# A vision transformer tower: probability transposes by row halves, exponential ahead of one eviction, value mask on VectorE

## The chip, the cores and the metric

The kernel runs on one core of a Trainium2 chip. The metric is device time in microseconds (us) of one execution; the time before is the median of three. The profile is that of one further execution. Engines are named as in the profile: PE is TensorE's matmul array, PEld its weight load, DVE is VectorE, ACT is ScalarE, POOL is GpSimd, SP is SyncE.

## What is computed

64 images of 96x96 pixels become 37 tokens each (36 patches and a class token) of 256 features. Two layers follow, each an attention and a feed-forward block, both with a layer norm ahead and a residual. Layer 0's feed-forward block has a shared expert and seven routed ones, layer 1's is dense. The change touches attention alone, which is, for layer 0 (layer 1 has no relative bias and no biases on q, k and v):

```python
q, k, v = split(layernorm(h) @ Wqkv + bqkv)          # 16 heads of 16
attn = einsum('bhtd,bhsd->bhts', q, k) / sqrt(16) + rel_bias   # -inf above the diagonal
attn = softmax(attn, axis=-1)
out = einsum('bhts,bhsd->bhtd', attn, v)
h = h + out @ Wout + bout
```

## The kernel before

**Staging.** Embedding, attention 0, shared feed-forward 0 with routing, routed experts over 43 tiles, attention 1 and feed-forward 1 run one after another. The residual stream `h` stays in SBUF, features on partitions, tokens in columns. An attention stage walks over 8 groups of 8 images (296 tokens); a group has four slots of two images (74 tokens), numbered n = 4g + p.

**A slot.** TensorE multiplies queries with masked keys for the 16 heads (`scores`, L1285). The result has image 0's 37 query rows at partitions 0 to 36 and image 1's at 64 to 100, and 16 x 37 columns (head, key). VectorE scales it and adds the bias (L841), takes the maximum (L847) and subtracts it (`centred`, L852); ScalarE takes the exponential into `Pr` (`exps`, L607). TensorE transposes `Pr` head pair by head pair (`probs_t`, L1308): eight transposes, each 128 rows by 74 columns, with the 128x128 identity as the moving operand. A result has 74 rows (head of the pair, key) and 128 columns, of which the 37 at 0 and the 37 at 64 are queries. ScalarE copies those into `PTs` (L616). `outputs` (L1316) multiplies `PTs` with `pairsum`, a 74x32 matrix of two blocks of ones (row sums, the softmax's denominators), and with the values `Vb`. ScalarE turns the sums into reciprocals by Ln and Exp (`shares`, L618), and VectorE multiplies (`normalise`, L861).

**Values.** The value projection of a group comes out of a bank with features on partitions. ScalarE evicts each of its two chunks by two activations (L603): into `VT[:, c, :, 0]` times a column `vmask[:, 0]`, which is 1 where the feature belongs to an even head and 0 elsewhere, and into `VT[:, c, :, 1]` with the mask of the odd heads. The bias is `val_b`, masked by a product on GpSimd at the start (L403). TensorE transposes them (`values`, L1299), four transposes a slot, to 74 rows (even or odd head, key) by 256 features for each image, and VectorE copies them into `Vb` (L859). The zeros of the mask let one 74-row product serve a pair of heads.

**Order.** Nothing is scheduled at run time. Each engine has a `step` that writes out its order for a group, and the engines wait on counting semaphores. Between its own four slots a step holds the projections of the next group (`project`, k = 0 and 1 keys, 2 and 3 queries, 4 and 5 values), the layer norm of the one after it (`mean`, `variance`; ScalarE's `squares` and `deviation`; GpSimd's `norm`; `upper_x` on ScalarE, L574, and `lower_x` on GpSimd, L395, which split a matrix into two parts for a product in three matmuls), and the output projection of the group before. In layer 1 a step also adds the routed experts' rows (`routed_out`, L1342, called the merge below). On TensorE the order of a body group is:

- slot 0: `probs_t(n)`, (merge), `scores`, values, projections 0 and 1, `outputs(n)`
- slot 1: `probs_t(n+1)`, mean, `scores`, values, projections 2 and 3, `outputs(n+1)`
- slot 2: `probs_t(n+2)`, output projection, `scores`, values, variance, projection 4, `outputs(n+2)`
- slot 3: `probs_t(n+3)`, output projection, `scores`, projection 5, `outputs(n+3)`, values of the next group's first slot

On ScalarE (L665) a slot is `shares` of the slot before, `probs_t`'s eviction, other work, the evictions of the slot's projections, and then the exponential of the next slot. The steps are 0, six in the middle and the last, which has no projections; the second last is `near`, where the layer norm ahead is that of the feed-forward block.

**Banks.** The eight PSUM banks are shared out by a fixed list (L1682). Scores lie in banks 0 and 1, transposed probabilities in 4 and 5, four head pairs in each (L1312). The other four rotate over values, projections, outputs, mean and variance; before TensorE writes one, `read_out` (L1256) waits for its last reader.

## Time and profile before

| | |
|---|---|
| median of 3 runs | 1243.29 us (1242.9 to 1245.18) |
| the profiled execution | 1245.89 us, its span 1244.0 us |
| PE busy | 1078.6 us (87%) |
| DVE, ACT, POOL busy | 616.9, 631.2, 396.8 us |
| attention 0, attention 1 | about 80 to 260 us, 905 to 1095 us from the span's start |

A row of the page's groups gives line, engine, operation, output and inputs with their forms and the count, then busy time and the mean duration in ns, then the idle time of the engine just before and what ended it. A timeline row gives start and duration in us; where several instructions are merged, the count stands at its end, and the duration runs from the first one's start to the last one's end. In brackets is the idle time ahead of it and the engine, tile and line that ended it.

### The profile page before, as it was taken

The page shows a single profiled execution, that of the slowest core. Times are in us where ns is not written, and L with a number is a line of the kernel's source. Part 1 is how long each engine was busy: PE and PEld are TensorE (multiplying, and loading weights), DVE is VectorE, ACT ScalarE, POOL GpSimd, SP SyncE. Part 2 cuts the span into 40 slices and gives each one's busy share as a digit, 9 for nine tenths or more (in the row PEclk, how much of TensorE's full clock was granted, in tenths as well). Part 3 has the DMA queues.
Part 4 walks back from the last instruction along what each step waited for, and adds up shares of the span by engine and source line. Part 5 has one row for each costly group of instructions (what it writes and reads, how often), then busy time and mean ns, then how long its engine had stood idle before and what let it go on. Part 6 is the DMA issues. An engine that isn't in the chain of part 4 may idle for free.

```text
span 1244.0 us, 27330 instructions
## 1 busy us (share of the span) xinstructions
PE 1078.6 (87%) x9892; PEld 913.4 (73%) x9893; DVE 616.9 (50%) x1174; ACT 631.2 (51%) x1067; POOL 396.8 (32%) x272
## 2 busy tenths in 40 slices
PE   6988888879988886999999999990578888869998
PEld 5877777767766664888888888880467777659998
DVE  3236665553332324566666666650156666624443
ACT  3446666643443432555555555550276566635554
POOL 2143434414544433012222222211456555341110
PEclk9999999988998988999999999995689999989999
DMA  6550000044111113011111111103100000000000
GB/s 226 186 216 2 2 0 1 3 162 151 27 23 23 24 20 93 22 34 34 34 34 34 34 34 34 33 27 98 56 27 28 33 1 2 3 1 21 16 13 30
DMA packets 30806, 57.25 MB, mean 46 GB/s; under 512 B 12892, under 2 KB 22314, under 8 KB 29588
## 3 DMA queue, kind: packets, MB, share of 16 engines
q1 hardware_dynamic: 16184, 44.06, 10.2%
q0 software_dynamic: 13328, 10.66, 3.3%
q10 hardware_dynamic: 1228, 1.61, 0.4%
q8 instruction: 47, 0.77, 0.3%
q14 instruction: 19, 0.16, 0.0%
HBM read 41.52 MB, written 14.67 MB: 45 GB/s over the span
## 4 chain that ended last, share of the span: by engine, by line
PE 68%; POOL 9%; ACT 9%; issue 8%; DMA 3%; DVE 2%; SPq 0%; ACTq 0%; POOLq 0%; DVEq 0%
PE ps L1193 22%; PE ps L1198 12%; PE ps L1200 11%; PE ps L1199 11%; POOL routed_in L458 6%; PE ps L1312 5%; ACT prs L610 2%; PE ps L1304 2%; PE ps L1569 2%; ACT vts L603 2%; DMA yg<-routed_out 1%; POOL xn L389 1%; ACT QT L598 1%; PE ps L1552 1%; ACT lnv L568 1%
## 5 line engine op out<-in xcount | busy, mean ns | idle before, releaser
L482 POOL DMA_INDIRECT routed_out<-yt,tile_to x43 | 65.7, 1528 | 290.4 <-DVE yt L1128 290.4
L1106 DVE TENSOR_TENSOR tile_w<-arena,tile_w 128x1408 fp32r<-128x1408 f32 x86 | 139.3, 1621 | 36.1 <-ACT tile_w L782 36.1
L1193 PE MATMUL ps<-arena,shared 128*128 x516 | 130.9, 395 | 1.0 <-ACT shared L778 1.0
L1198 PE MATMUL ps<-tile_w,xTs 128*128 128x352 f32 x344 | 120.0, 349 | 3.0 <-DVE xTs L1111 3.0
L782 ACT ACTIVATE tile_w<-arena 128x1408 fp32r x86 | 118.3, 1377 | 7.5 <-issue 7.5
L945 DVE TENSOR_TENSOR Hd<-Sg,ps 128x296 f32<-128x296 f32 x96 | 44.4, 462 | 148.5 <-ACT Sg L723 139.7
L771 ACT ACTIVATE shared<-ps 128x352 f32<-128x352 f32 x86 | 40.0, 465 | 145.7 <-PE ps L1200 141.2
L1200 PE MATMUL ps<-tile_w,xTs 128*128 128x352 f32 x344 | 112.1, 326 | 0.0
L1199 PE MATMUL ps<-tile_w,xTs 128*128 128x352 f32 x344 | 111.8, 325 | 0.0
L1193 PEld LDWEIGHTS ps<-arena,shared 128*128 128x128 f32 x516 | 90.8, 189 | 27.9 <-issue 15.6
L1193 PE MATMUL ps<-xn,shared 128*128 128x296 f32 x352 | 108.6, 455 | 0.0
L389 POOL TENSOR_TENSOR xn<-cen,rsd 128x592 f32<-128x592 f32 x32 | 46.4, 1451 | 190.7 <-ACT rsd L570 190.5
L1312 PE MATMUL ps<-cst,prs 128*74 128x128 f32 x512 | 68.4, 277 | 41.6 <-ACT prs L610 41.5
L379 POOL TENSOR_TENSOR Km<-KT,cst 128x592 f32<-128x592 f32 x64 | 86.4, 1352 | 45.9 <-ACT KT L598 24.4
L723 ACT ACTIVATE Sg<-ps 128x296 f32<-128x296 f32 x96 | 39.9, 415 | 114.1 <-PE ps L1193 65.8
L1193 PEld LDWEIGHTS ps<-xn,shared 128*128 128x128 f32 x352 | 72.9, 212 | 25.9 <-issue 9.3
L1312 PEld LDWEIGHTS ps<-cst,prs 128*74 128x74 f32 x512 | 51.7, 116 | 50.9 <-ACT prs L610 48.1
L866 DVE TENSOR_TENSOR OTn<-ps,RTs 128x148 f32<-128x148 f32 x64 | 20.0, 313 | 118.6 <-ACT RTs L624 118.6
L1198 PEld LDWEIGHTS ps<-tile_w,xTs 128*128 128x128 f32 x344 | 65.4, 190 | 17.1 <-issue 15.8
L1198 PE MATMUL ps<-xa_hi,qkv_p_lo 128*128 128x296 f32 x192 | 66.7, 348 | 3.5 <-POOL xa_lo L395 3.0
L852 DVE TENSOR_TENSOR Sb<-Sb,mx 128x592 f32<-128x592 f32 x64 | 66.5, 1039 | 0.3
L1199 PEld LDWEIGHTS ps<-tile_w,xTs 128*128 128x128 f32 x344 | 65.6, 191 | 0.0
(196 smaller groups left out, 2701.4 us busy)
## 6 DMA issues: line engine op xcount, KB each, us to landing
arena<-in_ew_dram SPq DMA_DIRECT2D x7, 2176.0 KB
x_in<-in_xT_dram SPq DMA_DIRECT2D x7, 888.0 KB, 4.9
xt<-routed_in SPq DMA_DIRECT2D x43, 129.0 KB, 2.0
yg<-routed_out SPq DMA_DIRECT2D x8, 592.0 KB
out_dram<-h SPq DMA_DIRECT2D x8, 296.0 KB, 2.7
routed_in<-zero_x SPq DMA_DIRECT2D x13, 129.0 KB, 10.5
gu_i<-in_gu_dram SPq DMA_DIRECT2D x1, 1536.0 KB, 20.9
shared<-in_gu_dram SPq DMA_DIRECT2D x1, 1408.0 KB, 7.4
```

Source lines behind the costliest of these rows:

```text
L379: pool.tensor_tensor(Km[p % 2], src, headmask.unsqueeze(1).unsqueeze(3).to_broadcast([P, DK, HG, W2]), ALU.mult).then_inc(a.km, 1)
L389: pool.tensor_tensor(xn[b][:], cen[:], rsd[:].unsqueeze(1).to_broadcast([P, DK, N]), ALU.mult).then_inc(s.xn, 1)
L458: pool.indirect_dma_start(xs, bass.IndirectOffsetOnAxis(slot[b][:, k, p:p + 1], 0), rows_x[b][:, p, k, :], None).then_inc(s_scat, 16)
L482: pool.indirect_dma_start(ys, bass.IndirectOffsetOnAxis(tile_to[b][:, 0:1], 0), yt[b][:], None).then_inc(s_yt, 16)
L782: act.activation(tile_w[half][0], gate_up_of(w, half), ACT.Copy).then_inc(s.wh, 1)
L852: dve.tensor_tensor(Sb[b], Sb[b], mx[b][:].unsqueeze(2).to_broadcast([P, HEADS, T]), ALU.subtract).then_inc(a.sc, 1)
L1106: dve.tensor_tensor(tile_w[half][1], gate_up_of(w, half), tile_w[half][0].bitcast(F32), ALU.subtract).then_inc(s.wl, 1)
L1193: return pe.matmul(out_, lhsT, rhs, start=start, stop=stop)
L1198: pe.matmul(out_, w[1], x[0], start=start, stop=False)
L1199: pe.matmul(out_, w[0], x[1], start=False, stop=False)
L1200: return pe.matmul(out_, w[0], x[0], start=False, stop=stop)
L1312: ins = pe.transpose(ps[0:W2, 4 + hp // 4, hp % 4 * P:(hp % 4 + 1) * P], Pr[p % 2][:, 2 * hp:2 * hp + 2, :].rearrange("p a k -> p (a k)"), ...
```

## The change

Four edits, none of which changes the result.

1. `probs_t` on TensorE makes 16 transposes instead of 8. Each head pair is transposed by row halves, 64 rows (one image) by 74 columns with a 64x64 identity as the moving operand; image 0's results go to bank 4, image 1's to bank 5, 64 columns for each head pair. A semaphore increment stands ahead of them, as it does ahead of the scores. ScalarE's eviction reads the new layout into the same `PTs`.
2. In each slot ScalarE's `exps` moves ahead of the slot's last projection eviction: ahead of projections 1, 3, 4 and 5 in slots 0 to 3.
3. A value chunk is evicted by one activation instead of two: it reads its bank twice (a broadcast dimension) and writes both halves of `VT`, with the plain bias and no mask.
4. The mask is applied where the transposed values leave the bank: VectorE's copy into `Vb` becomes a multiplication by `pairsum`, broadcast over head pairs and images. `vmask`, `val_b`, its product on GpSimd and the wait for it go.

```diff
                 pool.wait_ge(s_upper, 2 * l + 2)
                 pool.tensor_tensor(qkv_p[1], (qkv_w, qkv_w1)[l], qkv_p[0].bitcast(F32), ALU.subtract).then_inc(s_lower, 1)
                 pool.tensor_tensor(out_p[1], (out_w, out_w1)[l], out_p[0].bitcast(F32), ALU.subtract).then_inc(s_lower, 1)
-                if l == 0:
-                    pool.tensor_tensor(val_b[:], qkv_b[:, 2 * DK:].unsqueeze(2).to_broadcast([P, DK, 2]),
-                                       vmask.unsqueeze(1).to_broadcast([P, DK, 2]), ALU.mult).then_inc(s_val_b, 1)
                 for buf_free in (a.xn, a.km, a.OTs, F[l].xn) + ((F[l].sent,) if l == 0 else ()):
                     pool.sem_inc(buf_free, FREE)
                 norm(a, 0, 0)
...
                         act.activation((KT, QT)[k // DK][:, k % DK], src, ACT.Identity,
                                        bias=qkv_b[:, c:c + 1] if l == 0 else zero_t[:]).then_inc(a.proj, 1)
                     else:
-                        c = k - 2 * DK
-                        for odd in range(2):
-                            ins = act.activation(VT[:, c, :, odd], src.rearrange("p (i t) -> p i t", t=T), ACT.Identity, scale=vmask[:, odd:odd + 1],
-                                                 bias=val_b[:, c, odd:odd + 1] if l == 0 else zero_t[:])
-                        ins.then_inc(a.proj, 1)
+                        twice = src.rearrange("p (i t) -> p i t", t=T).unsqueeze(2).to_broadcast([P, GI, 2, T])
+                        act.activation(VT[:, k - 2 * DK], twice, ACT.Identity,
+                                       bias=qkv_b[:, k:k + 1] if l == 0 else zero_t[:]).then_inc(a.proj, 1)
 
                 def exps(n, p):
                     act.wait_ge(a.sc, FREE + n + 1)
...
                 def probs_t(n, p):
                     act.wait_ge(a.PT_mm, FREE + n + 1)
                     act.wait_ge(a.O_mm, n + 1)
-                    src = ps[0:W2, 4:6, :].rearrange("p b (h i q) -> p (b h) i q", h=HP // 2, i=2)[:, :, :, 0:T]
-                    act.activation(PTs[p % 2].rearrange("p h (i q) -> p h i q", i=2), src, ACT.Copy).then_inc(a.PTs, 1)
+                    src = ps[0:W2, 4:6, :].rearrange("p i (h q) -> p i h q", h=HP)[:, :, :, 0:T]
+                    act.activation(PTs[p % 2].rearrange("p h (i q) -> p i h q", i=2), src, ACT.Copy).then_inc(a.PTs, 1)
 
                 def shares(n, p, bk):
 
...
                         dequantise_gate_up()
                     if not X.last:
                         project(g + 1, 0, X.bank("proj0"))
+                    exps(n + 1, 1)
+                    if not X.last:
                         project(g + 1, 1, X.bank("proj1"))
-                    exps(n + 1, 1)
 
                     shares(n, 0, X.bank("O0"))
                     probs_t(n + 1, 1)
...
                     if not X.last:
                         project(g + 1, 2, X.bank("proj2"))
                         squares(*norm_ahead(l, g, X))
+                    exps(n + 2, 2)
+                    if not X.last:
                         project(g + 1, 3, X.bank("proj3"))
-                    exps(n + 2, 2)
 
                     shares(n + 1, 1, X.bank("O1"))
                     probs_t(n + 2, 2)
...
                         dequantise_down()
                     if not X.last:
                         deviation(*norm_ahead(l, g, X), X.bank("var"))
+                    exps(n + 3, 3)
+                    if not X.last:
                         project(g + 1, 4, X.bank("proj4"))
-                    exps(n + 3, 3)
 
                     shares(n + 2, 2, X.bank("O2"))
                     probs_t(n + 3, 3)
...
                             upper_x(a, g + 2, b, xa[b])
                         elif l == 1:
                             upper_x(F[1], 0, 0, xf1[0])
+                        exps(n + 4, 0)
                         project(g + 1, 5, X.bank("proj5"))
-                        exps(n + 4, 0)
                 over_body(act, l, step)
                 shares(4 * GROUPS - 1, 3, last.bank("O3"))
                 upper_out(GROUPS - 1, 1)
...
 
                     dve.wait_ge(a.V_mm, n + 1)
                     dve.wait_ge(a.O_mm, n + 1)
-                    dve.tensor_copy(Vb[p % 2][:].rearrange("p i d -> p (i d)"), ps[0:W2, bk, :]).then_inc(a.Vb, 1)
+                    by_pair = lambda t: t.rearrange("p (x d) -> p x d", d=2 * HD)
+                    dve.tensor_tensor(by_pair(Vb[p % 2][:].rearrange("p i d -> p (i d)")), by_pair(ps[0:W2, bk, :]),
+                                      pairsum.unsqueeze(1).to_broadcast([W2, 2 * HP, 2 * HD]), ALU.mult).then_inc(a.Vb, 1)
 
                 def normalise(g, n, p, gb, bk):
                     dve.wait_ge(a.RTs, FREE + n + 1)
...
                 def probs_t(n, p):
                     pe.wait_ge(a.ex, FREE + n + 1)
                     pe.wait_ge(a.PTs, FREE + n)
+                    pe.sem_inc(s_scores, 1)
                     for hp in range(HP):
-                        ins = pe.transpose(ps[0:W2, 4 + hp // 4, hp % 4 * P:(hp % 4 + 1) * P],
-                                           Pr[p % 2][:, 2 * hp:2 * hp + 2, :].rearrange("p a k -> p (a k)"), ident)
+                        for i in range(2):
+                            rows = slice(i * R64, (i + 1) * R64)
+                            ins = pe.transpose(ps[0:W2, 4 + i, hp * R64:(hp + 1) * R64],
+                                               Pr[p % 2][rows, 2 * hp:2 * hp + 2, :].rearrange("p a k -> p (a k)"),
+                                               ident[rows, rows])
                     ins.then_inc(a.PT_mm, 1)
 
                 def outputs(n, p, bk):
```

The hunks left out remove the declarations of `vmask`, `val_b` and its semaphore, and the wait for it.

## Rows read from the trace of the kernel before

**Rows 1.** The page: shares of the engines, and the probability transposes' group.

```profile
PE 1078.6 (87%) x9892; PEld 913.4 (73%) x9893; DVE 616.9 (50%) x1174; ACT 631.2 (51%) x1067; POOL 396.8 (32%) x272
L1312 PE MATMUL ps<-cst,prs 128*74 128x128 f32 x512 | 68.4, 277 | 41.6 <-ACT prs L610 41.5
```

**Rows 2.** The stretch view, one body group: start:end, length, busy time by engine (instructions), clock, DMA.

```profile
198.60:222.50 23.90, 20.87 (x362) 17.10 (x361) 13.71 (x23) 14.63 (x30) 10.60 (x8) 1.00 0.01 2
```

**Rows 3.** Timeline of TensorE: start, duration, what; the probability transposes of each slot.

```profile
198.64 1.07 PE L1312 MATMUL ps<-cst,prs 128*74 128x128 f32 x8
204.05 1.07 PE L1312 MATMUL ps<-cst,prs 128*74 128x128 f32 x8 [0.49 <-ACT prs L610]
210.32 1.07 PE L1312 MATMUL ps<-cst,prs 128*74 128x128 f32 x8 [0.67 <-ACT prs L610]
217.17 1.07 PE L1312 MATMUL ps<-cst,prs 128*74 128x128 f32 x8 [1.24 <-ACT prs L610]
222.48 1.07 PE L1312 MATMUL ps<-cst,prs 128*74 128x128 f32 x8
...
980.75 1.06 PE L1312 MATMUL ps<-cst,prs 128*74 128x128 f32 x8
1004.86 1.07 PE L1312 MATMUL ps<-cst,prs 128*74 128x128 f32 x8
```

**Rows 4.** Timeline of TensorE: other work of the same group, last row from layer 1.

```profile
200.97 0.40 PE L1198 MATMUL ps<-xa_hi,qkv_p_lo 128*128 128x296 f32 x1
...
203.08 0.48 PE L1193 MATMUL ps<-PTs,Vb 74*32 74x37 f32 x32
...
206.05 0.72 PE L1193 MATMUL ps<-Km,QT 64*37 64x148 f32 x16
206.70 0.63 PE L1304 MATMUL ps<-cst,vts 128*74 128x128 f32 x4
...
213.26 1.16 PE L1193 MATMUL ps<-squ,cst 128*128 128x296 f32 x4
...
957.53 0.68 PE L1342 MATMUL ps<-cst,yg 74*128 74x74 f32 x8
```

**Rows 5.** Timeline of ScalarE in the same group.

```profile
214.47 0.51 ACT L568 ACTIVATE lnv<-ps,eps_t 128x296 f32<-128x296 f32 x1 [2.38 <-PE ps L1193]
...
215.46 1.07 ACT L603 ACTIVATE vts<-ps,val_b,cst 128x296 f32<-128x296 f32 x2
216.43 0.69 ACT L610 ACTIVATE prs<-Sb 128x592 f32<-128x592 f32 x1
...
222.32 0.38 ACT L622 ACTIVATE RTs<-ps,zero_t 128x148 f32<-128x148 f32 x1
```

**Rows 6.** Timelines of GpSimd and VectorE, slot 3 of two groups of layer 0.

```profile
195.75 1.45 POOL L395 TENSOR_TENSOR xa_lo<-xn,xa_hi 128x592 fp32r<-128x592 f32 x1 [1.37 <-ACT xa_hi L574]
195.81 2.02 DVE L852 TENSOR_TENSOR Sb<-Sb,mx 128x592 f32<-128x592 f32 x1
...
219.54 0.77 DVE L852 TENSOR_TENSOR Sb<-Sb,mx 128x592 f32<-128x592 f32 x1
219.60 2.03 POOL L395 TENSOR_TENSOR xa_lo<-xn,xa_hi 128x592 fp32r<-128x592 f32 x1 [1.39 <-ACT xa_hi L574]
```

**Rows 7.** Groups by line, forms kept apart: busy, mean ns | idle before.

```profile
L616 ACT ACTIVATE PTs<-ps 74x592 f32<-74x592 f32 x64 | 42.4, 662 | 30.3 <-PE ps L1312 30.3
L859 DVE COPY Vb<-ps 74x512 f32<-74x512 f32 x64 | 43.5, 679 | 2.3 <-PE ps L1304 2.3
...
L847 DVE TENSOR_REDUCE mx<-Sb 128x16 f32<-128x592 f32 x64 | 48.6, 760 | 0.1
...
L872 DVE SCALAR_TENSOR_TENSOR h<-ps,out_b,h 128x296 f32<-128x296 f32 x16 | 8.4, 526 | 13.5 <-PE ps L1200 13.5
...
L866 DVE TENSOR_TENSOR OTn<-ps,RTs 128x148 f32<-128x148 f32 x64 | 20.0, 313 | 118.6 <-ACT RTs L624 118.6
```

More of the change, by code:

```diff
@@ L80, in vit_kernel @@
         headmask, prio = CONST.of(cst, "headmask"), CONST.of(cst, "prio")
-        vmask, pairsum = CONST.of(cst, "vmask"), CONST.of(cst, "pairsum")[0:W2]
+        pairsum = CONST.of(cst, "pairsum")[0:W2]
         region0, token2 = CONST.of(cst, "region0"), CONST.of(cst, "token2")
@@ L140, in vit_kernel @@
         qkv_b = sb("qkv_b", [P, 3 * DK])
-        val_b = sb("val_b", [P, DK, 2])
         out_b = [sb(f"out_b{l}", [P, DK]) for l in range(2)]
@@ L225, in vit_kernel @@
              for l in range(2)]
-        s_val_b, s_scores = sem("s_val_b"), sem("s_scores")
+        s_scores = sem("s_scores")
         ffn_sems = "mean_mm var_mm gu_mm dn_mm cen squ lnv rsd xn xh xl sg hd hh hl y"
@@ L654, in attention @@
                     embedding_out(GROUPS - 1, 1)
-                    act.wait_ge(s_val_b, 1)
                 squares(a, 1)
@@ L1636, in of @@
         return tensor[:, a:a + w]
-CONST = Packed(ident=P, mean=P, ones=P, before=W2, headmask=HG, vmask=2, pairsum=2 * HD, prio=PAIRS * EXPERTS, region0=EXPERTS, token2=PAIRS * 2,
+CONST = Packed(ident=P, mean=P, ones=P, before=W2, headmask=HG, pairsum=2 * HD, prio=PAIRS * EXPERTS, region0=EXPERTS, token2=PAIRS * 2,
                k128=KT_MAX, tri=EXPERTS * EXPERTS, tile_no=TILES, tile_row=TILES)
@@ L1733 @@
     CONST.of(consts, "pairsum")[0:W2] = np.kron(np.eye(2), np.ones((T, HD)))
-    CONST.of(consts, "vmask")[np.arange(P), np.arange(P) // HD % 2] = 1.0
     CONST.of(consts, "prio")[:] = np.tile(EXPERTS - np.arange(EXPERTS), PAIRS)
```

## The prediction, made before the changed kernel was run

> **What bounds the kernel now.** I read the busy shares first: TensorE is busy 87% of the span, the three other compute engines half or less [rows 1]. The change touches only the two attention stages, so the question is what ends last inside one of their groups. The stretch view shows that TensorE is granted its full clock, 1.00 or 2.4 GHz, through such a group and that nothing in it loads the DMA queues [rows 2]; the time there is a matter of order. A group has four slots, each beginning with the probability transposes. Their starts give the slots' lengths in a body group of layer 0: 5.41, 6.27, 6.85 and 5.31 us, 23.84 in all (198.64 to 222.48); a group of layer 1 takes 24.11 [rows 3]. Three of the four starts wait for ScalarE's exponential, and TensorE's matmul array is idle before them for 0.49, 0.67 and 1.24 us; the fourth has no such wait. So attention is a loop over two engines: projection matmul, its eviction on ScalarE, exponential on ScalarE, transposes on TensorE. The wait before slot 3's transposes is the longest because the two value evictions lie before that exponential [rows 3, 5].
>
> **The change, part by part.** I write each slot as its old length with what leaves or enters the chain that ends last.
>
> *Transposes.* Eight transposes with 128 moving columns take 1.07 us [rows 3], the last of them 0.28 by the mean of the 512 [rows 1], so they step at (1.07 - 0.28)/7 = 0.113 and hold the array 0.90 us. Sixteen with 64 columns hold it as long if they run in turn: the eight merge transposes with 74 moving columns step at (0.68 - 0.23)/7 = 0.065, so sixteen would take 1.03 [rows 4]. But the two halves lie in different array rows and write different banks, as the score matmuls do: 16 of those, 148 columns each, take 0.72 with a last one of 0.29, so they step at 0.029, though 148 columns cost 0.12 one after another by the rate of the variance matmuls ((1.16 - 0.42)/3 = 0.247 for 296 columns) [rows 4]. They overlap fourfold, two ways in rows and two in columns. Two ways in rows gives 8 x 0.057 = 0.46; the weight loads, now 16 instead of 8, may hold it up a little. I take 0.50, with bounds of 0.46 and 1.03, because the score matmuls are the nearest row. Against that stands a new change between the whole array and a half of it behind the block, where a mean, an output projection or the merge follows. The last score matmul starts at 206.05 + 15 x 0.029 = 206.49 and holds its tile 0.12; the value transposes start at 206.70, so such a change costs about 0.1 [rows 4]. I take 0.12 (bounds 0 and 0.2). Net, what follows the block comes 0.29 earlier in slot 1 and, where the loads of the next product now overlap the block's end, 0.21 in slots 2 and 3.
>
> The Trainium skill, "TensorEngine Tiling (Array Packing)", section Restrictions and Gotchas, wants different row tiles in different banks, and the diff does that (bank 4 + i). Its section Key Properties says that changing the tiling mode drains the engine; the 0.1 above is what this trace shows for that.
>
> *Slot 2.* The variance matmuls start 2.94 after the slot; 1.21 later ScalarE takes the logarithm, then two value activations hold it 0.97 (215.46 to 216.43), the exponential follows, and the next transposes start 0.74 behind that: 2.94 + 3.91 = 6.85 [rows 3 to 5]. With the exponential ahead of the eviction, 0.97 leaves the chain, and 0.21 with the shorter transposes: 5.67. TensorE's own work (variance at 2.73, projection 0.78 on, outputs 1.12 on, 0.70 for these) would be through at 5.33, so ScalarE still ends last.
>
> *Slot 1.* Here the eviction moved behind is an ordinary one of 296 elements, 0.51 as the logarithm of as many; activations in ScalarE's queue overlap by 0.1 (the value pair of 1.07 gives way after 0.97) [rows 5], so 0.40. 6.27 - 0.40 - 0.29 = 5.58. TensorE is through at about 5.2.
>
> *Slot 0.* Projection 0 starts 2.33 after the slot (200.97) [rows 4], held by VectorE's value copy, which follows the normalisation, which follows the denominators (Ln and Exp) on ScalarE. Those start 0.16 before the slot's transposes today (222.32 against 222.48) [rows 3, 5]. In the new order they directly follow the value eviction that the value transposes wait for: eviction about 0.70, 0.12 until TensorE starts, value transposes 0.49, and ScalarE free 0.10 before the eviction's end, so the denominators start about 0.69 to 0.71 ahead. Projection 0 comes 0.53 earlier, at 1.80. Its successor's wait (0.49) is gone as well: the exponential no longer waits for the eviction of projection 1, and TensorE goes from projection 0 through the outputs (203.56) in some 2.53 [rows 4]. New: 4.33. In layer 1 the merge's transposes stand between and keep TensorE busy, so projection 0 can gain only the 0.29: a group there saves 0.3 less.
>
> *Value mask.* The two activations of a value eviction, 1.07 [rows 5], become one of 592 elements. A 592-element activation out of a bank takes 0.66 [rows 7]; upper bound 0.77 (0.38 for 148 elements and 0.51 for 296 make 0.88 ns an element, so 0.51 + 0.26) [rows 5]. I take 0.70. On VectorE a copy of 512 elements out of the bank, 0.68, becomes a multiply with a second operand; the residual is such an operation, 0.53 for 296 elements [rows 7], which scales to 0.92 at most. I take 0.69, as the copy's length is by its elements, and it is hidden: VectorE is busy 13.7 of 23.9 us [rows 2]; with its cover gone it would cost 0.01 to 0.24 a slot. The GpSimd product that goes ran once.
>
> *Slot 3, where the swap can hurt.* The value eviction of projection 5 gates the value transposes, and these stand before the next slot's transposes on TensorE. The swap puts it behind an exponential that waits for VectorE's centring. Today the centring starts at 195.81 and takes 2.02 instead of 0.77, since GpSimd's lower-part subtraction began at 195.75 and runs till 197.20; in the group after it VectorE is first by the same 0.06 (219.54, 219.60) and GpSimd takes the 2.03 [rows 6]. This costs nothing today, since the exponential is last in ScalarE's queue. From now on it does. In the new schedule both engines follow the denominators of slot 2. The exponential starts 0.74 before the slot, the value eviction 0.15 before it, the denominators 0.51 after it, and their two activations (0.38 and about as much again) end at 1.34. GpSimd's operation starts after the probability eviction (0.66) and the upper part (as long by elements, 0.69), each overlapped by 0.1 [rows 7]: from 1.24 on 0.56 + 0.69 + 0.06 = 2.55. VectorE's centring starts after normalisation (0.31), maximum (0.76) and residual (0.53), each overlapped by 0.09 [rows 7]: from 1.38 on 0.22 + 0.67 + 0.44, about 2.73. GpSimd is first by 0.18 and the centring ends at 2.55 + 1.45 + 0.63 = 4.63. Exponential 4.67, eviction 5.26, value transposes 6.08, next slot 6.57 (5.31 today). Without the collision: 5.45.
>
> The Trainium skill, "SBUF — State Buffer", section Who interferes with whom, says that a VectorE instruction with two SBUF inputs and a GpSimd one exclude each other for their whole length, the earlier one going first. Both pairs of rows 6 agree. It also says that one SBUF input doesn't collide, so the new multiply would not.
>
> *Sum.* Body group of layer 0: 4.33 + 5.58 + 5.67 + 6.57 = 22.15 against 23.84: 1.7 saved. Layer 1, 0.3 less: 1.4 of its 24.11 [rows 3]. Five such groups each: 8.5 and 7.0. The second last step of layer 0 has no upper part and so no collision: 2.8; that of layer 1, without a merge but with one: 1.7. The first steps, filled by other waits, I take at 1.5 each, the last ones (no projections, shorter transposes alone) at 1.0. Together 8.5 + 2.8 + 2.5 + 7.0 + 1.7 + 2.5 = 25.0 us. The profiled execution took 1245.89 (span 1244.0) and would take 1220.9; it stood 2.6 above the median of 1243.29, so the time to expect is 1218. Nothing behind attention waits for anything but attention's end, so the gain should reach the end of the span.
>
> **Rivals.**
> *No collision.* VectorE is first in slot 3. 0.18 is a small lead, and 0.06 decided it both ways. Saves 1.12 more in 11 groups: 1206. For it: the lead hangs on the eviction's exact length. Chance 0.2.
> *The halves do not overlap.* Transposes hold the array 1.03. Then slot 0 gives back 0.36, slots 1 and 2 0.53 each, slot 3 nothing in the collided chain: 0.4 left per group of layer 0, 0.1 to 0.2 in layer 1, with the first and last steps some 6: 1237. For it: twice as many weight loads, each still 74 columns wide. Against it: the score matmuls' 0.029. Chance 0.14. The Trainium skill, "TensorE: Matmul & The Clock Gate", section LDWEIGHTS, says that a load's time goes with columns and not rows, columns divided by 1.2 ns; sixteen would take 0.99 by it, this rival's time. Its figure is too high for this trace, where merge transposes with 128 weight columns step at 0.065 and not 0.107 [rows 4].
> *Slower.* Loads of a half are exposed and each transpose costs as much as a whole one does, 0.113: 1.81 for the block. Slots 0 to 2 then each lose about 1.3 against my forecast, slot 3 some 0.7, because projection 5 comes later: 26.8 against 23.84, so 1243 + 13 x 3.0 = 1282. It decides from a block of about 1.15 us on. Chance 0.04.
> *The change doesn't do what it says:* ScalarE arrives at the exponential before VectorE has centred in slots 0 to 2 too, and the swap is worth nothing there; only the transposes remain, 0.2 to 0.3 a slot, eaten by slot 3: within 3 us of 1243. Against it: the exponential of slot 2 starts right behind the value pair, with no wait for VectorE [rows 5], and there are two to three microseconds of idle VectorE in each slot by rows 2. Chance 0.05.
>
> **How the numbers follow.** Forecast with the collision 0.57 (own range 1210 to 1228). The range of 8 in 10 takes in the case without collision and most of the serial halves: 1203 to 1236. Bounds of the sum: evictions 0.66 or 0.77 move a group by 0.1, the change of tiling by 0.3, together 5 us. About 0.2% (2.5 us) is what measurement can tell from no change. Faster 0.91, same 0.04, slower 0.05.
>
> **What would show it.** A block of sixteen transposes that lasts 0.65 to 0.75 us (a last one of 0.22 and a step near 0.03); no wait for the exponential before slot 1, 0.3 before slots 2 and 3; slot lengths near 4.3, 5.6, 5.7 and 6.6; centring in slot 3 at 2.0 us and a wait of the value transposes for the value eviction there. A block over 1 us, or slot 3 near 5.4, would make me wrong in size; a slot 3 over 8 us in sign.

## The result and the profile after

The changed kernel took 1249.78 us in the median of 19 runs (1243.88 to 1252.59), the kernel before 1244.33 in 19 runs beside it (1241.28 to 1248.04): a ratio of 1.0041, 95% interval 1.0029 to 1.0054. The prediction was 1218, with a range up to 1236. It was wrong in sign. The profiled execution took 1247.23 with a span of 1245.4, against 1245.89 and 1244.0 before. The profiled runs are thus 1.3 apart and the medians 5.4; the account below is of the profiled runs alone, and what the slower runs of the changed kernel do besides is not shown.

The page of the kernel after, its shares and the groups that answer to [rows 1] and [rows 7], and the queue that brings TensorE's instructions:

```profile
PE 1077.7 (87%) x10404; PEld 909.5 (73%) x10405; DVE 627.0 (50%) x1174; ACT 615.1 (49%) x1035; POOL 390.6 (31%) x271
q8 instruction: 59, 0.97, 0.3%
L1302 PE MATMUL ps<-cst,vts 128*74 128x128 f32 x256 | 46.3, 311 | 27.4 <-ACT vts L598 27.4
L1313 PE MATMUL ps<-cst,prs 64*74 64x64 f32 x1024 | 44.1, 228 | 26.3 <-ACT prs L604 19.9
```

The transposes now wait 19.9 us for the exponential where they waited 41.5, but the value transposes wait 27.4 for their eviction. The queue q8 moved 59 packets; the page of before has 47. That it brings TensorE's instructions is read from the runs: it is 59 in every kernel with 512 or more matmuls added, 48 with 256 added and 47 with none.

The stretch view of a body group of layer 0, one row for each slot (columns as in [rows 2]):

```profile
201.47:207.13 5.66, 5.66 (x99) 4.80 (x98) 3.63 (x6) 2.82 (x6) 1.72 (x1) 0.70 0.00 0
207.13:212.85 5.72, 5.36 (x107) 4.27 (x102) 3.63 (x6) 3.20 (x8) 2.95 (x2) 1.00 0.01 3
212.85:218.57 5.72, 5.38 (x100) 4.38 (x101) 3.38 (x6) 3.28 (x8) 0.66 (x1) 1.00 0.01 3
218.57:225.14 6.57, 4.54 (x97) 3.61 (x97) 3.95 (x5) 4.30 (x9) 5.07 (x4) 1.00 0.01 2
```

The group takes 23.67 against 23.84. Slots 1, 2 and 3 are where the prediction had them (5.58, 5.67, 6.57). Slot 0 is not: 5.66 against 4.33, with TensorE busy all through and a granted clock of 0.70. TensorE's timeline around its start shows why, and the start of slot 1 stands beside it:

```profile
200.91 0.63 PE L1302 MATMUL ps<-cst,vts 128*74 128x128 f32 x4 [1.94 <-ACT vts L598]
201.47 0.64 PE L1313 MATMUL ps<-cst,prs 64*74 64x64 f32 x16
202.05 1.10 PE L1191 MATMUL ps<-Km,QT 64*37 64x148 f32 x16
203.08 1.07 PE L1302 MATMUL ps<-cst,vts 128*74 128x128 f32 x4
...
207.13 0.64 PE L1313 MATMUL ps<-cst,prs 64*74 64x64 f32 x16
...
208.89 0.72 PE L1191 MATMUL ps<-Km,QT 64*37 64x148 f32 x16
209.54 0.63 PE L1302 MATMUL ps<-cst,vts 128*74 128x128 f32 x4
```

After 1.94 us without work the transposes still run at their usual length. The score matmuls then take 1.10 instead of 0.72 and the value transposes 1.07 instead of 0.63. The stretch view in short pieces gives the clock:

```profile
195.00:198.90 3.90, 3.90 (x92) 3.19 (x92) 2.69 (x4) 2.28 (x5) 3.42 (x4) 1.00 0.02 4
198.90:200.90 2.00, 0.07 (x7) 0.00 (x0) 1.27 (x2) 1.38 (x3) 1.62 (x1) 1.00 0.00 0
200.90:202.90 2.00, 1.99 (x36) 1.42 (x36) 1.29 (x3) 1.39 (x4) 0.00 (x0) 0.83 0.00 0
202.90:204.90 2.00, 2.00 (x12) 1.74 (x9) 1.69 (x4) 0.51 (x1) 1.42 (x1) 0.50 0.00 0
204.90:206.40 1.50, 1.50 (x9) 1.36 (x8) 0.65 (x1) 0.74 (x2) 0.30 (x1) 0.75 0.00 0
206.40:207.20 0.80, 0.80 (x51) 0.72 (x52) 0.00 (x0) 0.75 (x2) 0.00 (x0) 1.00 0.00 0
```

1.00 is 2.4 GHz and 0.50 is 1.2 GHz. The engine had been idle for some two microseconds, the clock fell behind that (after the transposes, by the lengths above), and it came back while the projections ran. The Trainium skill, "TensorE: Matmul & The Clock Gate", section HAM oscillation, warns in general terms that a wait between bursts of matmuls lets the clock drop, so that the next burst starts slowly. That is what this trace shows, behind an idle time of 1.94; the prediction did not weigh it.

The kernel before shows the same thing once in attention 0, in a row that the prediction did not look at. Its first slot stands behind a wait of 2.17 (TensorE's timeline):

```profile
79.48 1.10 PE L1312 MATMUL ps<-cst,prs 128*74 128x128 f32 x8 [2.17 <-ACT prs L610]
80.51 1.22 PE L1193 MATMUL ps<-Km,QT 64*37 64x148 f32 x16
```

The scores take 1.22 there and not 0.72. The slot takes 6.60, at a granted clock of 0.74, against 5.41 in a body group at 1.00; it belongs to the first step, so not all of the difference need be the clock's.

A second loss occurs once, at the start of the fourth group of attention 0 (TensorE's timeline):

```profile
146.97 0.63 PE L1302 MATMUL ps<-cst,vts 128*74 128x128 f32 x4 [1.95 <-ACT vts L598]
151.05 0.29 PE L1313 MATMUL ps<-cst,prs 64*74 64x64 f32 x1 [3.45 <-issue]
154.23 1.01 PE L1313 MATMUL ps<-cst,prs 64*74 64x64 f32 x15 [2.89 <-issue]
```

TensorE stands still for 3.45 + 2.89 = 6.34 us and waits for nothing the profile shows. This is where TensorE's loop over the groups (two passes of two groups, steps 1 to 4) branches back.

*The account.* Two causes are added up here: the low clock in slot 0 and the stall at the branch. From the first probability transposes of attention 0 to the last took 177.82 before and 179.57 after, +1.75 where I expected -13.8. The stall lengthens two slots, to 10.04 (the slot 3 before it, others 6.5 to 6.7) and 8.87 (slot 0, others 5.66), together 6.6. Against 4.33, slot 0 at the low clock costs 0.80, 1.12 and four times 1.3 in six groups, 7.2 (the fourth 1.3 is in the stalled slot 0, counted above only from 5.66 on), and slot 3 of the second last step, 6.29, is 0.8 longer than what I had for it (23.86 - 2.8 for the group, less the three other slots, 5.48). That makes 14.6 of the 15.5. In attention 1 the same stretch took 183.30 and 182.32, -0.98 where I expected -11: its slots 0 are the longest, since the merge's transposes lie in the slow stretch too (7.58 and 7.77 in two groups, 6.30 and 6.33 in two more, 5.6 before). One group escapes: behind a wait of 2.10, the longest of all, its slot 0 takes 4.78 at a clock of 1.00.

### The profile page after: what moved, and what is told of

The parts are those of the page before. It is cut to its first block, busy times and chain, and to the rows that moved or that the text cites. A ratio compares the mean times of both kernels' runs of the same rounds, so it can differ in the third digit from the quotient of the medians.

```text
span 1245.4 us, 28328 instructions
## 1 busy us (share of the span) xinstructions
PE 1077.7 (87%) x10404; PEld 909.5 (73%) x10405; DVE 627.0 (50%) x1174; ACT 615.1 (49%) x1035; POOL 390.6 (31%) x271
## 4 chain that ended last, share of the span: by engine, by line
PE 64%; POOL 10%; issue 9%; ACT 7%; DVE 5%; DMA 4%; SPq 0%; ACTq 0%; DVEq 0%; POOLq 0%
PE ps L1191 23%; PE ps L1196 11%; PE ps L1198 10%; PE ps L1197 10%; POOL routed_in L454 6%; PE ps L1302 3%; DVE Sb L848 3%; PE ps L1313 2%; PE ps L1571 2%; ACT prs L604 2%; ACT vts L598 1%; DMA x_in<-in_xT_dram 1%; DMA yg<-routed_out 1%; POOL xn L388 1%; PE ps L1554 1%
## 5 line engine op out<-in xcount | busy, mean ns | idle before, releaser
L378 POOL TENSOR_TENSOR Km<-KT,cst 128x592 f32<-128x592 f32 x64 | 87.1, 1363 | 57.9 <-ACT KT L594 46.3
L848 DVE TENSOR_TENSOR Sb<-Sb,mx 128x592 f32<-128x592 f32 x64 | 78.4, 1225 | 0.3
L1196 PE MATMUL ps<-xa_hi,qkv_p_lo 128*128 128x296 f32 x192 | 70.6, 368 | 3.6 <-POOL xa_lo L394 3.6
L1302 PE MATMUL ps<-cst,vts 128*74 128x128 f32 x256 | 46.3, 311 | 27.4 <-ACT vts L598 27.4
L1313 PE MATMUL ps<-cst,prs 64*74 64x64 f32 x1024 | 44.1, 228 | 26.3 <-ACT prs L604 19.9
```

Source lines behind the costliest of these rows:

```text
L378: pool.tensor_tensor(Km[p % 2], src, headmask.unsqueeze(1).unsqueeze(3).to_broadcast([P, DK, HG, W2]), ALU.mult).then_inc(a.km, 1)
L848: dve.tensor_tensor(Sb[b], Sb[b], mx[b][:].unsqueeze(2).to_broadcast([P, HEADS, T]), ALU.subtract).then_inc(a.sc, 1)
L1196: pe.matmul(out_, w[1], x[0], start=start, stop=False)
L1302: ins = pe.transpose(ps[0:W2, bk, i * D + c * P:i * D + (c + 1) * P], VT[:, c, 2 * p + i].rearrange("p a k -> p (a k)"), ident)
L1313: ins = pe.transpose(ps[0:W2, 4 + i, hp * R64:(hp + 1) * R64], Pr[p % 2][rows, 2 * hp:2 * hp + 2, :].rearrange("p a k -> p (a k)"), ident[ ...
```

## The experiments

The theory was: (A) the swap in slot 3 leaves TensorE idle long enough for its clock to fall, and that costs slot 0 its gain; (B) the stall at the loop's branch comes with the added instructions. The rivals: the row halves are slow for another reason, or slot 0 is limited by ScalarE, or the stall belongs to the new order. All ratios are to the kernel before, run beside each kernel (medians 1244.6 to 1245.6). Diffs are against the changed kernel unless said otherwise.

**1. Slot 3 in the old order, the rest as changed.**

```diff
-                        exps(n + 4, 0)
                         project(5, g + 1)
+                        exps(n + 4, 0)
```

> The changed kernel with one edit: in slot 3 the exponential of the next slot stands behind the fifth projection's eviction again. Theory (the swap puts the value eviction behind a late centring, TensorE idles 1.94 us there, its clock falls to half and slot 0 takes 5.7 to 6.6 instead of 4.3): the value transposes wait under 0.6 us, granted clock 1.00 in attention, slot 3 about 5.3 and slot 0 about 4.9 us, period near 21.7, time 1215 to 1222. Rival (the 6.3 us in which TensorE waits for nothing shown, once in attention 0, and the larger instruction traffic eat the gain, whatever slot 3 does): the time stays above 1238. Second rival (slot 0 is long because of the new multiply on VectorE or the new eviction): slot 0 stays at 5.7 or more with the clock at 1.00.

Measured: 1222.89 (1222.74 to 1223.75), ratio 0.9815 [0.9799, 0.9832]. A late group of layer 0 takes 21.62, with a slot 0 of 4.79 and a slot 3 of 5.39. The stall is there (3.73 and 2.91). One moved call was worth 27 us. The time is just above the 1215 to 1222 expected.

**2. Centring ahead of the residual in slot 3.** The exponential stays ahead of the eviction, but VectorE comes to its input before GpSimd starts.

```diff
+                        centred(n + 4, 0)
                         ...
-                        centred(n + 4, 0)
```

> The changed kernel with one edit on VectorE: in slot 3 the centring stands ahead of the residual, so that it starts some 0.3 us before GpSimd's subtraction instead of 0.16 behind it. The swap stays. Theory: the centring takes 0.77 instead of 1.93, GpSimd's subtraction takes the delay (about 2.0), the value transposes wait about 0.4 us, clock 1.00, slot 3 about 4.9, slot 0 about 4.3, period near 20.6, time 1203 to 1212. Rival (instruction fetch): above 1238. Rival (the swap itself is at fault, not the collision): slot 3 stays near 6.5.

Measured: 1217.66 (1215.38 to 1217.86), ratio 0.9766 [0.975, 0.9783]. The centring and GpSimd's subtraction, the exponential behind it, the value transposes behind that (timelines of VectorE, GpSimd, ScalarE and TensorE):

```profile
210.70 0.77 DVE L848 TENSOR_TENSOR Sb<-Sb,mx 128x592 f32<-128x592 f32 x1
...
210.86 1.93 POOL L394 TENSOR_TENSOR xa_lo<-xn,xa_hi 128x592 fp32r<-128x592 f32 x1 [0.50 <-ACT xa_hi L570]
...
211.50 0.70 ACT L604 ACTIVATE prs<-Sb 128x592 f32<-128x592 f32 x1 [0.72 <-DVE Sb L848]
...
212.99 0.60 PE L1301 MATMUL ps<-cst,vts 128*74 128x128 f32 x4 [0.54 <-ACT vts L598]
```

A lead of 0.16 us turns the centring from 1.93 into 0.77. TensorE's wait falls from about 2.0 to 0.54, slot 3 takes 5.04 to 5.10 and slot 0, at full clock, 4.24 to 4.38. I had expected 1203 to 1212; the stall (3.22 and 2.42) is still there. Both orders that shorten TensorE's idle time keep slot 0 short.

**3. The wait filled, everything else as changed.** Six matmul instructions on constants (three products of two each), their result unused, stand before the value transposes in slot 3.

```diff
+                def fill(g, bk):
+                    for k in range(3):
+                        mm(ps[:, bk, 0:N], ident, cst[:, 0:N])
...
-                        at("V0n", values, n + 4, g + 1, 0)
+                        at("V0n", fill, g)
+                        values(n + 4, g + 1, 0, X.bank("V0n"))
```

> The changed kernel with three extra matmuls (identity by 296 columns of constants, about 1.5 us) into the bank of the value transposes, just before TensorE waits for the value eviction in slot 3; their results are overwritten. Nothing else moves. Theory (the clock falls because of the idle stretch): slot 3 stays at 6.6, the clock stays at 1.00, and slot 0 falls from 5.7 or 6.6 to about 4.4, period near 22.4, time 1222 to 1232. Rival (slot 0 is long for another reason than the clock): no slot gets shorter, time at or above the changed kernel's, 1245 to 1252.

Measured: 1227.01 (1224.27 to 1228.87), ratio 0.9848 [0.9827, 0.9869]. TensorE's timeline and the stretch view of slot 0:

```profile
188.09 1.76 PE L1191 MATMUL ps<-cst 128*128 128x296 f32 x6
190.11 0.63 PE L1302 MATMUL ps<-cst,vts 128*74 128x128 f32 x4 [0.26 <-ACT vts L598]
190.67 0.64 PE L1313 MATMUL ps<-cst,prs 64*74 64x64 f32 x16
...
194.97 0.64 PE L1313 MATMUL ps<-cst,prs 64*74 64x64 f32 x16
...
190.67:194.97 4.30, 4.30 (x97) 3.58 (x96) 3.54 (x6) 2.76 (x6) 1.74 (x1) 1.00 0.02 4
```

This settles A as far as the idle time goes. Slot 3 keeps its length (6.51) and its late eviction; only TensorE's idle time is gone. Slot 0 is 4.30 at a clock of 1.00. Useless work made the kernel 23 us faster than the changed one. The stall moved: none in attention 0, one of 3.68 in attention 1.

**4. Both edits (1 and 2).** 

> The changed kernel with both: exponential behind the fifth projection's eviction in slot 3, and centring ahead of the residual. Theory: with the collision gone the order of the two in slot 3 hardly matters, slot 3 about 4.8, slot 0 about 4.5 because the denominators start later than with the swap; period near 20.7, time within 5 us of the run that only moves the centring, 1203 to 1215. Rival (the swap in slot 3 costs by itself): more than 5 us faster than that run.

Measured: 1215.36 (1210.38 to 1217.51), ratio 0.9759 [0.9743, 0.9775]. The stall remains (3.37 and 2.74).

**5 to 8. One part of the change at a time**, built from the kernel before: the transposes alone (new `probs_t`, old order, old value mask); the swap alone in all four slots; the swap in slots 0 to 2; the value mask alone.

> The kernel before with the transposes by row halves alone (and ScalarE's eviction of their new layout). Theory: the block takes 0.64 as in the changed kernel; slots 1 and 2 get 0.15 to 0.25 shorter, slot 0 stays at 5.4 since VectorE's value copy holds it, slot 3 gets 0.2 shorter; clock 1.00; about 0.6 us a group or 9 in all. Against it stands TensorE's fetch stall of about 6.5 us, which I expect here because the instructions are added here: 1238 to 1243 with it, 1232 to 1236 without. Rival (the transposes bring most of the 28 us that the run with both edits gained): under 1228.

Measured: 1248.72 (1245.98 to 1251.33), ratio 1.0033 [1.0019, 1.0047]. A body group of layer 0 is shorter, 23.42, but the stall is there, as a wait for nothing shown (TensorE's timeline):

```profile
152.41 0.29 PE L1315 MATMUL ps<-cst,prs 64*74 64x64 f32 x1 [3.69 <-issue]
155.31 1.01 PE L1315 MATMUL ps<-cst,prs 64*74 64x64 f32 x15 [2.61 <-issue]
```

So the stall does not belong to the new order. The time is above the 1238 to 1243 that I expected with the stall. Part of the miss is the clock again: in two groups of layer 1 it falls inside slot 3, which takes 6.76 and 6.66 against 5.10 to 5.31 in the others. The wait ahead was only 1.32 (TensorE's timeline, the first of the two):

```profile
953.34 0.64 PE L1315 MATMUL ps<-cst,prs 64*74 64x64 f32 x16 [1.32 <-ACT prs L610]
...
955.42 1.22 PE L1193 MATMUL ps<-Km,QT 64*37 64x148 f32 x16
```

In the other groups of that stage waits of 1.31 and 1.32 leave the clock at full. The rest of the miss is open.

> The kernel before with the exponential ahead of the last eviction in all four slots, nothing else. Theory: slots 1 and 2 at 5.9, but in slot 3 the value pair (1.07) stands behind the late centring, TensorE idles over 2 us, slot 3 is near 7.0, the clock falls, and slot 0 takes 5.8 or more; about as slow as the kernel before or slower, 1243 to 1258, with no fetch stall. Rival (the swap gains in every slot and something else lost it): under 1230.

Measured: 1253.93 (1249.22 to 1256.93), ratio 1.0064 [1.0044, 1.0084]. No halves, no stall, 47 packets on q8, and still slower than before: the order alone suffices. Here the value transposes wait about 2.5 us in the body groups. Slot 3 takes 7.2 to 7.6, which eats what slots 0 to 2 gain, so that a group of layer 0 at full clock takes 23.44 or 23.83, about as before (23.92); those in which the clock falls take 24.8 to 26.0. The stretch view of slot 0 in four groups of layer 0, and in TensorE's timeline the wait before the second and the fourth of them:

```profile
101.54:106.05 4.51, 4.51 (x90) 3.87 (x88) 3.55 (x6) 2.70 (x6) 1.62 (x2) 1.00 0.02 4
124.98:129.50 4.52, 4.52 (x91) 3.88 (x89) 3.55 (x6) 2.78 (x6) 1.48 (x1) 1.00 0.03 5
148.81:155.63 6.82, 6.82 (x89) 5.46 (x87) 3.47 (x6) 2.56 (x5) 1.45 (x1) 0.63 0.00 0
199.97:206.81 6.84, 6.84 (x90) 5.48 (x88) 3.47 (x6) 2.65 (x5) 1.45 (x1) 0.63 0.01 2
...
124.52 0.63 PE L1307 MATMUL ps<-cst,vts 128*74 128x128 f32 x4 [2.46 <-ACT vts L603]
...
199.11 1.07 PE L1307 MATMUL ps<-cst,vts 128*74 128x128 f32 x4 [2.45 <-ACT vts L603]
```

The same slot with the same instructions takes 4.5 at full clock and 6.8 at 0.63. And the same wait, 2.46 and 2.45, is once without and once with the fall. The traces don't show what decides between them.

> The kernel before with the exponential ahead of the last eviction in slots 0, 1 and 2 alone; slot 3, transposes and mask as before. Theory: slot 1 loses 0.40 (5.9), slot 2 loses 0.97 (5.9), slot 0 loses 0.3 to 0.5 (the value copy still holds projection 0), slot 3 stays at 5.3 to 5.4; clock 1.00, no fetch stall; about 1.75 a group over 13 groups, 1218 to 1224. Rival (the gain needs the shorter transposes): above 1232.

Measured: 1227.09 (1225.83 to 1228.72), ratio 0.9865 [0.9851, 0.9879]. Groups of 22.35 in layer 0 (slots 4.87, 5.87, 5.87, 5.73) and 23.0 in layer 1. This is the part of the change that pays most. I had expected 1218 to 1224, with a slot 3 of 5.3 to 5.4; with 5.73 to 5.81 it is some 0.4 longer, and there the exponential waits 0.30 for the late centring (see 13).

> The kernel before with the single value activation and the mask on VectorE alone. Theory: the pair that held ScalarE 0.97 becomes one of 0.74 that holds it 0.64; slots 2 and 3 lose 0.33 each, VectorE's multiply takes 0.68 as the copy did; 0.66 a group, 1233 to 1237. Rival (reading the bank twice or multiplying costs as much as it saves): 1241 to 1246.

Measured: 1236.72 (1236.19 to 1237.24), ratio 0.9938 [0.9924, 0.9953]. The multiply takes 0.68, as the copy did; the gain is ScalarE's, 0.35 in slot 2 (6.50 against 6.85) where the value pair stood before the exponential, and 0.33 in slot 3 (4.98 against 5.31) in the groups in which the centring isn't late. Where it is late, slot 3 keeps 5.37.

**9 to 11. What of it is worth keeping.** Whole transposes with both edits; both edits with the halves in slots 1 and 2 only; experiment 2 with whole transposes. The edit of the second:

```diff
-                    pe.sem_inc(s_scores, 1)
-                    for hp in range(HP):
+                    if p in (1, 2):
+                        pe.sem_inc(s_scores, 1)
+                        for hp in range(HP):
...
+                    else:
+                        for hp in range(HP):
+                            ins = pe.transpose(ps[0:W2, 4 + hp // 4, hp % 4 * P:(hp % 4 + 1) * P],
```

> The run with both edits, with the eight whole transposes of before in place of the sixteen halves. Theory (the sixteen halves bring TensorE's fetch stall of 6.3 us and some time at half clock behind it, once in attention 0): the stall is gone, the block takes 1.07 again, groups get 0.5 to 0.7 longer (21.7 instead of 21.1), which over 12 groups costs about what the stall did: 1212 to 1219. Rival (the stall is not tied to the halves): it stays, and the time is 1221 to 1226.

Measured: 1216.14 (1212.29 to 1217.67), ratio 0.976 [0.9745, 0.9776]; no stall, 47 packets. Groups are longer than with the halves (21.6 against 21.1 in layer 0, 22.25 against 21.45 in layer 1), and yet the time is that of experiment 4. The halves' gain and the stall with its slow clock cancel: 0.5 and 0.8 in some five groups each against two slots of 8.17 and 8.86 where others take 4.9 and 4.8.

> The run with both edits, with halves in slots 1 and 2 only, whole transposes in slots 0 and 3; half as many instructions added. Theory (the stall depends on how many instructions TensorE's loop has): either it is gone, then 1208 to 1213, with groups of about 21.4, or it is there whole, then 1216 to 1220. Rival (the stall belongs to the row halves themselves and not to their number, so it would halve): about 3 us once.

Measured: 1210.05 (1205.56 to 1216.79), ratio 0.9725 [0.9701, 0.9749], the fastest kernel here: groups of 21.2 in layer 0 and 21.4 to 21.48 in layer 1, no stall, 48 packets. Its lead over experiments 4 and 9 is not quite clear of noise: its interval just overlaps theirs. With half of the added instructions the stall is gone and most of the gain stays.

> As the run with both edits and whole transposes, but with the exponential ahead of the fifth projection's eviction in slot 3 as well. Tells what the swap in slot 3 is worth when VectorE is first. Theory: slot 3 gets about 0.1 to 0.2 longer and slot 0 about 0.4 shorter: a group of 21.4 against 21.7, 1209 to 1216, unless VectorE and GpSimd meet elsewhere. Rival (the swap in slot 3 costs by itself, by the idle TensorE ahead of the value transposes): slower than its twin by 3 us or more.

Measured: 1215.92 (1214.89 to 1218.81), ratio 0.9776 [0.976, 0.9792], the same as experiment 9. With the collision gone, the order of exponential and eviction in slot 3 makes no difference that the runs can tell.

**12. The whole transposes of experiment 9, each issued twice.** As many instructions as the changed kernel, but no halves.

```diff
-                    for hp in range(HP):
+                    for hp in 2 * list(range(HP)):
```

> The run with both edits and whole transposes, with each block of eight transposes issued twice into the same banks: as many instructions added to TensorE's loop as the halves add, but whole transposes, one kind of tile and no extra semaphore increment. Theory (the stall comes from the number of instructions in the loop): TensorE again waits for nothing shown for two stretches of about 3 us at the start of the fourth group of attention 0, and the instruction queue moves 59 packets instead of 47. The slots get 0.4 to 0.9 longer besides. Rival (the stall comes from the row halves, their tile change or their semaphore increment): no such stretch, 47 packets.

Measured: 1270.08 (2 runs), ratio 1.02 [1.0182, 1.0219]. Most of the 54 us over experiment 9 is the doubled work (a block takes 1.94 instead of 1.07, in 64 blocks); what counts is TensorE's timeline, and q8 moving 59 packets again:

```profile
156.56 0.64 PE L1309 MATMUL ps<-cst,prs 128*74 128x128 f32 x2 [3.10 <-issue]
```

The stall (3.10, then 2.34 at 159.54) comes with the added instructions and not with the row halves. The DMA view of the second pass of TensorE's loop shows it from the other side. First the kernel before, attention 0 from 150 to 198, then the one after, 150 to 199 (all packets; q8: packets, MB, share):

```profile
DMA packets 0, 0.00 MB, mean 0 GB/s; under 512 B 0, under 2 KB 0, under 8 KB 0
```

```profile
q8 instruction: 8, 0.13, 1.2%
```

Before, nothing at all is moved in this pass: it runs on instructions that are there already. After, eight packets come, one every six microseconds on average; they are eight of the twelve that q8 moved more. Experiment 3 has both cases in one kernel: its second pass in attention 0 (146 to 190), which has no stall, and that in attention 1 (963 to 1009), which has one:

```profile
DMA packets 0, 0.00 MB, mean 0 GB/s; under 512 B 0, under 2 KB 0, under 8 KB 0
...
q8 instruction: 7, 0.11, 1.1%
```

The same holds for the others I looked at: none on q8 in the second pass of attention 1 of the changed kernel, nor in attention 0 of experiments 9 (no halves) and 10, all without a stall; seven each in the transposes alone (152 to 199) and in the doubled transposes (156 to 203), both with one. The Trainium skill, "Runtime: NRT & Kernel Launch", section Instruction fetch mechanics, says that a taken branch to a block outside the window that the engine holds forces a fetch before it can go on. The traces agree: the stall stands at the branch, and only where q8 moves packets in the second pass. That page of the Trainium skill counts the window as two blocks; the kernel before ran a pass of 721 recorded matmuls and as many loads with nothing fetched, so for TensorE it is larger here. By the same page of the Trainium skill TensorE's buffer holds 2048 instructions in blocks of 256; the stretch view of after has 403 matmuls and 398 loads in a group, some 1600 for a pass of two, so it would fit or not according to where its blocks begin; this is an estimate. That the place of the code is what differs between the two attentions follows from this estimate alone and was not tried.

**13. The kernel before, with the centring of slot 3 ahead** (diff against the kernel before: the same move as in 2).

> The kernel before with the centring ahead of the residual in slot 3, nothing else. Theory: the collision of VectorE and GpSimd there goes, but nothing waits for the centring in the old order; slot 3 5.3 instead of 5.4 in the groups that collided, 0.1 in some ten groups, within 2 us of the kernel before. Rival (the late centring costs in the old order too, and its removal is what the edited kernels gained): under 1238.

Measured: 1245.26 (1242.95 to 1247.5, 12 runs), ratio 1.0004 [0.9993, 1.0016]. The centring takes 0.77 (VectorE's timeline), slot 3 stays at 5.31 to 5.39:

```profile
194.55 0.77 DVE L852 TENSOR_TENSOR Sb<-Sb,mx 128x592 f32<-128x592 f32 x1
```

So the collision was free in the kernel before, as the prediction said. But it is not the swap in slot 3 alone that gives it a price. Experiment 1 has slot 3 in the old order, and its exponential waits for the late centring (timelines of GpSimd, VectorE and ScalarE):

```profile
212.22 1.46 POOL L394 TENSOR_TENSOR xa_lo<-xn,xa_hi 128x592 fp32r<-128x592 f32 x1 [0.49 <-ACT xa_hi L570]
212.38 1.93 DVE L848 TENSOR_TENSOR Sb<-Sb,mx 128x592 f32<-128x592 f32 x1
...
214.34 0.70 ACT L604 ACTIVATE prs<-Sb 128x592 f32<-128x592 f32 x1 [0.44 <-DVE Sb L848]
```

Experiment 4 differs from it in the place of the centring alone: slot 3 takes 4.84 against 5.39, and the time is 1215.36 against 1222.89. The collision is free only as long as something else ends later than the centring. In the kernel before that was the pair of value activations; one activation in its place (mask alone) or the swaps ahead of it (slots 0 to 2) already let it show.

## Why the prediction was wrong, point by point

*Transposes: right.* The sixteen take 0.64 with a last one of 0.228, a step of (0.64 - 0.23)/15 = 0.027 where I took 0.029. The halves overlap, and a group with the transposes alone gains 0.42 (23.84 to 23.42), where the 0.29 and 0.21 that I took for slots 1 and 2 were measured as 0.14 and 0.16 (6.13 and 6.69): right in the mechanism, too high in what it saves. The rival of serial halves and that of exposed loads are out.

*Slots 1 and 2: right.* 5.72 and 5.72 against 5.58 and 5.67; slot 1 is longer by what the transposes save less there. The waits for the exponential are none, 0.36 and 0.35 in slots 1, 2 and 3, against none, 0.3 and 0.3. The rival that the swap does nothing is out: the swap in slots 0 to 2 alone is worth some 17 us.

*Value mask: right.* The eviction takes 0.736 (I took 0.70), the multiply 0.680 (0.69). The multiply is covered, as I had it; the eviction stands in the chain of slot 3, where the 0.04 is of no weight.

*Slot 3 and its collision: right in a body group.* GpSimd starts at 221.00, VectorE at 221.16 (0.16 apart, I had 0.18), the centring takes 1.93 and the slot 6.57, the very number. That it fits to the hundredth is luck: GpSimd starts 2.43 into the slot where I had 2.55, and the value transposes start at 6.04 and not 6.08. It rests on two rows of the changed kernel:

```profile
221.00 1.46 POOL L394 TENSOR_TENSOR xa_lo<-xn,xa_hi 128x592 fp32r<-128x592 f32 x1 [0.49 <-ACT xa_hi L570]
...
221.16 1.93 DVE L848 TENSOR_TENSOR Sb<-Sb,mx 128x592 f32<-128x592 f32 x1
```

Wrong was "no upper part and so no collision" for the second last step of layer 0. There GpSimd's masking of the keys (L378) starts at 244.66, VectorE's centring at 244.82 and takes 1.65; the slot is 6.29. I had looked only for the partner that collides today, and not at what else GpSimd would be doing at that moment.

*The step that failed first: slot 0.* The chain of slot 0, 4.33, was right at full clock: 4.30 in experiment 3. (Its last term is slightly off: the rows give 203.56 - 200.97 = 2.59 and not 2.53, which would make it 4.39.) But the sum took it from the row that says TensorE "is granted its full clock, 1.00 or 2.4 GHz, through such a group" [rows 2], and kept that for the group after. My own slot 3 contradicted it. It put the value transposes at 6.08 with no work ahead of them but what the slot of 5.31 had already held, so it had about 1.3 us of idle time more than before in one place, on top of the 0.49 that the value transposes waited there already. The longest idle time that the clock of [rows 2] had been seen with was 1.24 [rows 3]; after, it is 2.02 in that slot. What belonged there is a bound on both sides: the same slot at 1.2 GHz in part. The trace of before had a price for it, 6.60 against 5.41 at most, in the first slot of attention 0 behind a wait of 2.17. The low clock cost 1.3 in most groups of layer 0 and up to 3.0 in layer 1 (7.77 against 4.78), where the merge lies in the same stretch. With it, the change's gain per group of layer 0 fell from 1.7 to 0.2.

*The step that was missing: the instructions.* I counted the time of sixteen transposes and loads, not that 512 more of each have to be brought in. The added instructions turned a loop whose second pass brought in nothing into one that is fetched again (in attention 0; in attention 1, with as many added, it is not), 6.34 us at the branch and 6.6 with the slow clock behind it. "Nothing behind attention waits" was true, and the loss was inside.

*The rivals.* The case that ended on the slower side was the wrong one: it was made of exposed weight loads, a cost at TensorE's array. The real one needed the wait that I had forecast myself, plus the clock. Undoing that wait (experiments 1 and 2) gives 1222.9 and 1217.7. The case without a collision, which is experiment 2, I had at 1206; some 8 of the 12 us missing there are the stall and the slow clock behind it (slots of 8.33 and 9.22 where others take 5.04 and 4.3), the rest is open.

## What to carry to other kernels

When a reordering makes a wait longer on TensorE, even where the sum shows room for it, price the work behind the wait at the lower clock too: here about two microseconds of idle time cost 0.8 to 3.0 us in the following slot, in most cases but not in all. Look in the trace of before for a wait of that length and read what the work behind it took. When an edit shortens what covered a VectorE instruction with two inputs from SBUF, look up every GpSimd instruction that may start just before it. And count instructions in a hardware loop: if the instruction queue is silent in later passes before the change, ask whether it still will be.

## What the runs showed of the hardware

- The same idle time of TensorE (2.45 and 2.46) was followed by a clock of 0.63 over one slot 0 and 1.00 over another; in the changed kernel the fall came behind 1.94, and not behind 2.10 in one group. With the transposes alone it came behind 1.32 in two groups and not behind 1.31 and 1.32 in others.
- A loop that is fetched again stalls TensorE at its branch twice in a row, 3.45 and 2.89 (3.69 and 2.61, 3.10 and 2.34 in other kernels), with one or two transposes between; in one kernel there is a single stall of 3.68.
- Sixteen half-row transposes with 74 weight columns take 0.64 against 1.07 for eight whole ones, though they need twice as many weight loads.
- Which of VectorE's centring and GpSimd's subtraction starts first, by 0.06 to 0.16 us, decides which is stretched: 0.77 becomes 1.93 to 2.02 for the one, about 1.46 becomes 1.93 to 2.03 for the other.
